# LayerNorm, V and output projection, weight quantizer and x loads in the first stage of a transformer layer: other slots

## The chip, the cores and the metric

One Trainium2 chip, all 8 cores. Each core computes 8192 of the 65,536 tokens by itself, with its own copy of the weights; the cores exchange nothing. The metric is the device time in microseconds of the slowest core. The kernel before took 3341.05 us (median of 3 runs, 3340.89 to 3342.73).

## The reference, cut to what matters

One layer: LayerNorm, attention in windows of 128 tokens (each window sees itself and the one before), residual, LayerNorm, a gated FFN whose activations and weights are rounded to FP4 in blocks of 16.

```python
x = x + _L0_attn_ref(_layernorm(x), wq, wkv, wo, bo)
x = x + _L0_ffn_ref(_layernorm(x), w_gate, w_up, w_down)

def _L0_attn_ref(x, wq, wkv, wo, bo):        # H = 16 heads of 64, W = 128
    q = x @ wq;  k, v = split(x @ wkv, 2)
    # windows of 128; keys and values of the window before are put in front
    sim = einsum('bwid,bwjd->bwij', qw, kw) * 64 ** -0.5, causal mask
    out = einsum('bwij,bwjd->bwid', softmax(sim), vw)
    return out @ wo + bo

def fp4_quant_dequant(x):                    # blocks of 16
    scale = max(max(abs(xb)) / 6.0, 1e-12)
    q = _GRID[searchsorted(_MID, abs(xb / scale))] * sign * scale
def _L0_ffn_ref(x, w_gate, w_up, w_down):    # 1024 -> 2816 -> 1024
    h = silu(q(x) @ q(w_gate).T) * (q(x) @ q(w_up).T)
    return q(h) @ q(w_down).T
```

## The kernel before

Every engine has its own stream of instructions, in the order in which the Python code calls it. A token (semaphore, count) stands for an instruction that has ended; an instruction that needs tokens waits at the head of its engine's queue, and all behind it wait too. DMAs are issued from two queues: SP (plain loads and DMA transposes) and POOL (weight loads that turn float32 into bf16, and stores). The DMA queues are in order as well: a DMA whose token is missing holds the issue of all behind it.

`attention` runs first, then a fence, then `ffn`. The change touches `attention` alone. It handles 64 tiles T of 128 tokens in 16 chunks of 4 tiles (`cc`), and in each chunk 8 pairs of heads (`p`). One pass of the loop over `n = 8 * cc + p` is called a slot here: 128 slots and one more to drain. In a slot TensorE (PE) does for pair n: scores of two half chunks (L536 to L549), the Q and K projection of pair n+1 (L440), softmax weights times V of pair n-1 (L600, L602), and two groups of eight 512-column matmuls (L440) called `extra`: the V projection of a tile of the next chunk (`proj_v`, drained by ACT in L483) or the output projection of a tile of the chunk before (`proj_o`, drained by DVE in L495). VectorE (DVE) does the row maxima (L558, two in a slot, so the first of them marks a slot's start), drains K (L468), divides (L610, L613) and rounds weights. ScalarE (ACT) does the exponentials (L566), drains Q (L457) and V, and most of LayerNorm. SP transposes the softmax weights P (`turn_p`, L574), the attention output (`turn_ao`, L622) and normalized x (`turn_x`, L409) by DMA.

LayerNorm of a tile (LN1): `load_x` (L340) into one of two buffers, `square_sum` (L384) and `plain_sum` (L391) on ACT, `scalars` on POOL (11 small instructions for two tiles, L286 to L301), `normalize` (L402) on ACT, `turn_x` on SP. In chunk cc the tiles of chunk cc+2 are loaded and summed and two of them normalized; the other two are normalized in slots 0 and 1 of the next chunk. Tiles 0 to 7 are done ahead of slot 0.

The residual: `load_xr` (L503) loads x once more, `add_bo` (L510) adds the bias on POOL, `proj_o` adds the product, and POOL stores to `x1s` in DRAM (L498). Two buffers; `load_xr(T)` waits for the store of tile T-2.

The weight quantizer (`rounding`) rounds the FFN's weights during the attention stage: 136 jobs of 5 steps, 7 DVE instructions (L228 to L273) and an ACT square (L253) each, a load by SP (L638) and a store by POOL (L672). `fill(share)` runs it up to that share of its 680 steps: 3% ahead of slot 0, and from there in equal parts, five calls of `upto` in a slot, up to slot 126.

## Time and profile before

| | us |
|---|---|
| median of 3 runs | 3341.05 |
| the profiled execution | 3333.16 |
| its span, slowest core (core 6) | 3331.5 |
| spans of the 8 cores | 3320.3 to 3331.5 |
| attention, from the span's start to the last matmul of it | about 1389 |
| PE busy over the span | 2984.4 (90%) |
| DVE busy over the span | 2787.0 (84%) |
| ACT busy over the span | 1535.0 (46%) |

The profile is one execution on the slowest core. Each engine's busy time is the sum of its instructions; "idle before" names what ended the wait. A matmul's recorded end is modelled, so a group of PE instructions that waits in its middle can look long and not idle. The granted clock is the share of TensorE's 2.4 GHz that the chip gave in that stretch: 1.00 is 2.4 GHz, 0.50 is 1.2 GHz, and what lies between is a mixture of the two. All times below are microseconds from the span's start.

### The profile page before, as it was taken

The page shows a single profiled execution, that of the slowest core. Times are in us where ns is not written, and L with a number is a line of the kernel's source. Part 1 is how long each engine was busy: PE and PEld are TensorE (multiplying, and loading weights), DVE is VectorE, ACT ScalarE, POOL GpSimd, SP SyncE. Part 2 cuts the span into 40 slices and gives each one's busy share as a digit, 9 for nine tenths or more (in the row PEclk, how much of TensorE's full clock was granted, in tenths as well). Part 3 has the DMA queues.
Part 4 walks back from the last instruction along what each step waited for, and adds up shares of the span by engine and source line. Part 5 has one row for each costly group of instructions (what it writes and reads, how often), then busy time and mean ns, then how long its engine had stood idle before and what let it go on. Part 6 is the DMA issues. An engine that isn't in the chain of part 4 may idle for free.

```text
span 3331.5 us, 53061 instructions; the slowest of 8 cores (3320.3 to 3331.5 us)
## 1 busy us (share of the span) xinstructions
PE 2984.4 (90%) x16413; PEld 1407.5 (42%) x16736; DVE 2787.0 (84%) x4992; ACT 1535.0 (46%) x3018; POOL 1190.0 (36%) x1912
## 2 busy tenths in 40 slices
PE   2888888888899998438999999999999999999997
PEld 1333443344444444114444444444444444444443
DVE  1888888888888889239999999999999999999984
ACT  3666665566666664124343433433333443343331
POOL 2123222222223232214444444444444444444431
PEclk7899999999999999769999999999999999999998
DMA  9689888888888987765333333333333333333322
GB/s 175 146 194 197 203 189 189 190 197 195 198 204 200 205 198 171 175 128 127 88 93 93 93 90 87 88 93 93 93 87 93 87 90 93 93 93 87 88 77 71
DMA packets 818805, 445.59 MB, mean 134 GB/s; under 512 B 736352, under 2 KB 747616, under 8 KB 818528
## 3 DMA queue, kind: packets, MB, share of 16 engines
q1 hardware_dynamic: 782112, 348.83, 47.9%
q0 software_dynamic: 36416, 93.34, 9.2%
q8 instruction: 140, 2.29, 0.3%
q14 instruction: 137, 1.12, 0.1%
HBM read 186.19 MB, written 84.41 MB: 81 GB/s over the span
## 4 chain that ended last, share of the span: by engine, by line
PE 65%; DVE 11%; DMA 7%; SPq 7%; issue 5%; ACT 3%; POOL 2%; POOLq 0%; ACTq 0%; DVEq 0%
PE ps L914 35%; PE ps L928 18%; PE ps L440 10%; DMA bfar<-bfar 5%; DVE far L558 2%; ACT bfar L566 2%; DVE far L259 1%; SPq L622 1%; SPq L574 1%; DVE far L495 1%; DVE bfar L273 1%; SPq L859 1%; DVE far L246 1%; SPq L861 1%; DVE bfar L613 1%
## 5 line engine op out<-in xcount | busy, mean ns | idle before, releaser
L914 PE MATMUL ps<-bfar 128*128 128x512 bf16 x6016 | 1250.8, 362 | 102.3 <-DMA bfar<-bfar 90.0
L440 PE MATMUL ps<-bfar 128*128 128x512 bf16 x3949 | 978.8, 389 | 156.0 <-ACT bfar L457 76.4
L914 PEld LDWEIGHTS ps<-bfar 128*128 128x128 bf16 x6144 | 602.1, 98 | 729.0 <-issue 103.9
L1037 POOL TENSOR_TENSOR bfar<-bfar,far 128x512 bf16<-128x512 bf16 (+1 forms) x512 | 503.2, 1002 | 955.7 <-DVE far L1020 952.0
L928 PE MATMUL ps<-bfar 128*128 128x512 bf16 x2768 | 646.0, 380 | 8.4 <-DVE far L1052 5.9
L440 PEld LDWEIGHTS ps<-bfar 128*128 128x128 bf16 x4096 | 386.4, 99 | 552.9 <-issue 198.4
L952 ACT ACTIVATE far<-ps 128x512 f32<-128x512 f32 (+1 forms) x384 | 214.0, 557 | 848.8 <-PE ps L914 828.7
L566 ACT ACTIVATE bfar<-ps,far 128x256 bf16<-128x256 f32 x1024 | 423.2, 478 | 341.6 <-DVE far L558 341.2
L928 PEld LDWEIGHTS ps<-bfar 128*128 128x128 bf16 x2816 | 276.0, 98 | 327.2 <-issue 10.1
L969 ACT ACTIVATE far<-far 128x512 f32<-128x512 f32 (+1 forms) x512 | 289.8, 599 | 267.4 <-DVE far L1020 267.4
L993 DVE TENSOR_REDUCE far<-far 128x32 f32<-128x512 f32 (+1 forms) x512 | 308.3, 642 | 68.7 <-ACT far L959 68.7
L986 DVE TENSOR_TENSOR far<-far,ps 128x512 f32<-128x512 f32 (+1 forms) x384 | 238.0, 635 | 149.7 <-PE ps L914 145.7
L510 POOL TENSOR_TENSOR far<-far 128x1024 f32<-128x1024 f32 x64 | 154.3, 2411 | 572.6 <-DMA far<-x 416.3
L558 DVE TENSOR_REDUCE far<-ps 128x4 f32<-128x1024 f32 x256 | 311.4, 1216 | 16.9 <-PE ps L549 16.7
L1008 DVE SCALAR_TENSOR_TENSOR far<-far 128x512 f32<-128x512 f32 (+1 forms) x512 | 317.3, 660 | 0.0
L1015 DVE SCALAR_TENSOR_TENSOR bfar<-far 128x512 bf16<-128x512 f32 (+1 forms) x512 | 311.6, 649 | 0.0
L1020 DVE SCALAR_TENSOR_TENSOR far<-far 128x512 f32<-128x512 f32 (+1 forms) x512 | 311.4, 648 | 0.0
L259 DVE SCALAR_TENSOR_TENSOR far<-far 128x512 f32<-128x512 f32 (+1 forms) x136 | 111.5, 820 | 42.5 <-ACT far L253 42.2
L1003 DVE RECIPROCAL far<-far 128x64 f32<-128x64 f32 (+1 forms) x256 | 135.1, 528 | 8.8
L600 PE MATMUL ps<-bfar 128*128 128x65 bf16 x1024 | 97.9, 195 | 44.8 <-DMA bfar<-bfar 44.5
L228 DVE TENSOR_REDUCE far<-far 128x32 f32<-128x512 f32 (+1 forms) x136 | 89.8, 660 | 46.9 <-DMA far<-wgate 41.1
L495 DVE TENSOR_TENSOR far<-far,ps 128x512 f32<-128x512 f32 x128 | 86.8, 680 | 40.0 <-PE ps L440 20.8
(68 smaller groups left out, 2618.6 us busy)
## 6 DMA issues: line engine op xcount, KB each, us to landing
far<-x SPq DMA_DIRECT2D x128, 512.0 KB, 5.0
far<-x1s SPq DMA_DIRECT2D x128, 512.0 KB, 3.7
x1s<-far POOLq DMA_DIRECT2D x64, 512.0 KB, 3.9
out<-far POOLq DMA_DIRECT2D x64, 512.0 KB, 3.0
far<-wgate SPq DMA_DIRECT2D x44, 256.0 KB, 3.7
far<-wup SPq DMA_DIRECT2D x44, 256.0 KB, 4.0
bfar<-bfar SPq DMA_TRANSPOSE x700, 3.9
far<-wdown SPq DMA_DIRECT2D x40, 256.0 KB, 3.7
```

Of the source, the lines that this page charges most:

```text
L440: ins = e.matmul(c.p(col, [[1, 512]]), lhs(k), rhs(k), start=(k == 0), stop=(k == 7))
L558: t_max[(n, hf)] = dve.step(lambda e: e.tensor_reduce(out=c.f(NM + s * 4, [[1, 4], [1, 1]]), in_=c.p(PS_S + hf * 1024, [[256, 4], [1, 256] ...
L566: t_exp[(n, hf)] = act.step(lambda e, i=i: e.activation(out=c.b(A_P + s * 1024 + i * 256, [[1, 256]]), in_=c.p(PS_S + hf * 1024 + i * 256, ...
L914: ins = e.matmul(c.p(col, [[1, nw]]), c.b(xo + k * 128, [[1, 128]]), c.b(woff + k * FI + ns, [[1, nw]]), start=(k == 0), stop=(k == 7))
L928: ins = e.matmul(c.p(col + half * 512, [[1, 512]]), c.b(ho + k * 128, [[1, 128]]), c.b(WDQ + k * DM + half * 512, [[1, 512]]), start=(k == ...
L969: done_sq[sl] = act.step(lambda e, i=i, nw=nw: e.activation(out=c.f(Q_W + i * 512, [[1, nw]]), in_=c.f(Q_V + i * 512, [[1, nw]]), func=AF. ...
L986: t_h[n] = tok[i] = dve.step(lambda e, n=n, i=i, nw=nw, sl=sl: e.tensor_tensor(out=source(sl, i, nw, False), in0=c.f(G_SG + (n % 2) * 512, ...
L993: tok[i] = dve.step(lambda e, i=i, sl=sl: e.tensor_reduce(out=c.f(am + i * 32, [[1, nbs[i]], [1, 1]]), in_=source(sl, i, nbs[i] * 16, True ...
L1008: shifted[i] = dve.step(lambda e, i=i, nw=nw: e.scalar_tensor_tensor(out=c.f(Q_S + i * 512, [[1, nw]]), in0=c.f(Q_W + i * 512, [[1, nw]]), ...
L1015: done_r[sl] = dve.step(lambda e, i=i, nw=nw: e.scalar_tensor_tensor(out=c.b(F_R + i * 512, [[1, nw]]), in0=c.f(Q_W + i * 512, [[1, nw]]), ...
L1020: done_v[sl] = dve.step(lambda e, i=i, sl=sl: e.scalar_tensor_tensor(out=c.f(Q_V + i * 512, [[16, nbs[i]], [1, 16]]), in0=source(sl, i, nb ...
L1037: done_q[sl] = pool.step(lambda e, i=i, dst=dst, psc=psc, pb=pb: e.tensor_tensor(out=c.b(dst, [[16, pb], [1, 16]]), in0=c.b(F_R + i * 512, ...
```

## The change

Five things are edited, all in `attention`.

1. Ahead of slot 0 only tiles 0 to 3 are normalized. Tiles 4 to 7 (chunk 1) and 8, 9 (half of chunk 2) are summed and normalized in slots 0 to 5 of chunk 0, by a table (`plan`). All of x's tiles 4 to 7 are loaded ahead of slot 0, tiles 6 and 7 into the residual buffers.
2. The quantizer starts with slot 6 and ends with slot 126 as before.
3. The load of wo moves from the start to the end of slot 2.
4. `proj_v` moves from slots 0, 1, 4, 5 of a chunk to 1, 4, 5, 7, and `proj_o` from 2, 3, 6, 7 to 2, 3, 6 and slot 0 of the next chunk. `normalize` of slots 0 and 1 goes from the slot's middle to its end, and the transpose of a chunk's tile 1 from the end of slot 7 to the middle of slot 0.
5. The loads are dealt out, one in a slot: `load_x` in slots 0, 2, 4, 6 (before: 0, 1, 4, 5), `load_xr` in 1, 3, 5, 7 (before: 0, 1, 4, 5).

```diff
+    def aside(T):
+        return T in (2, 3, 6, 7)
     def load_x(T):
-        sem = s_x[T] if T in (2, 3) else s_x[T % 2]
-        free = t_xn.get(T - 4 if T in (4, 5) else T - 2) if T >= 4 else None
+        sem = s_x[T % 2 + 2 * aside(T)]
+        free = None if T < 4 else t_xn[T - 4] if T < 10 else t_xn[T - 2]
...
-    t_wo_w = load_w(A_WO, d["wo"], 0, DM, DM, s_c[3])
+    t_wo_w = {}
...
     for T in range(4):
         normalize(T)
         turn_x_pe(T)
-        if T < 2:
-            load_x(T + 4)
+        load_x(T + 4)
...
-    for T in (4, 5):
-        square_sum(T)
-        plain_sum(T)
-    scalars(4)
-    for T in (4, 5):
-        normalize(T)
-        turn_x(T)
-        load_x(T + 2)
-    for T in (6, 7):
-        square_sum(T)
-        plain_sum(T)
-    scalars(6)
-    head = 0.03
-    fill(head)
+    quiet = 6
...
-            fill(head + (1 - head) * min(1.0, (n + part) / (n_units - 2)))
+            fill(min(1.0, (n + part - quiet) / (n_units - 2 - quiet)))
...
-        if more and p in (0, 1, 4, 5):
-            T = base1 + {0: 0, 1: 1, 4: 2, 5: 3}[p]
+        if more and cc >= 1 and p in (1, 4, 5, 7):
+            T = base1 + {1: 0, 4: 1, 5: 2, 7: 3}[p]
             extra = [(proj_v, T, 0), (proj_v, T, 1)]
-        if live and p in (2, 3, 6, 7) and cc >= 1:
-            T = base1 - 8 + {2: 0, 3: 1, 6: 2, 7: 3}[p]
+        if live and p in (2, 3, 6) and cc >= 1:
+            T = base1 - 8 + {2: 0, 3: 1, 6: 2}[p]
             extra = [(proj_o, T, 0), (proj_o, T, 1)]
+        if p == 0 and cc >= 2:
+            extra = [(proj_o, base1 - 9, 0), (proj_o, base1 - 9, 1)]
         if p in (2, 3) and cc == 0:
             extra = [(proj_v, 2 * p - 4, 1), (proj_v, 2 * p - 3, 1)]
+        if p >= 4 and cc == 0:
+            extra = [(proj_v, p, 0), (proj_v, p, 1)]
...
+        if cc == 0 and live:
+            plan = {0: ((4,), (5,)), 1: ((), (6,)), 2: ((7,), ()), 3: ((), (8,)), 4: ((9,), ())}
...
+            if p in (1, 3, 5):
+                middle.append(lambda T=2 * p + {1: 2, 3: 0, 5: -2}[p]: rows(T, T + 1))
...
+            if p == 2:
+                t_wo_w[0] = load_w(A_WO, d["wo"], 0, DM, DM, s_c[3])
...
-        if ahead and p in (0, 1):
-            load_x(base2 + p)
-        if ahead and p in (4, 5):
-            load_x(base2 + p - 2)
+        if ahead and cc >= 1 and p % 2 == 0:
+            load_x(base2 + p // 2)
...
-        if live and p in (0, 1, 4, 5) and cc >= 1:
-            T = base1 - 8 + {0: 0, 1: 1, 4: 2, 5: 3}[p]
-            load_xr(T)
-            add_bo(T)
+        if live and p in (1, 3, 5, 7):
+            T = base1 - 8 + {7: 4, 1: 1, 3: 2, 5: 3}[p]
+            if 0 <= T < n_tiles - 4:
+                load_xr(T)
+                add_bo(T)
```

How the instructions stand on three engines. The changed kernel's lines lie 2 further down from L340 on (L558 is L560 there). VectorE at the start, from the drains of the transposed x tiles (L425) and of the first K projection (L468) on, before:

```order
L425 CAST bfar<-ps 128x8x128 x4
L468 CAST bfar<-ps 128x512
L228 TENSOR_REDUCE far<-far 128x32
L234 TENSOR_SCALAR far<-far 128x32
L240 RECIPROCAL far<-far 128x32
L246 SCALAR_TENSOR_TENSOR far<-far 128x512
...
L273 TENSOR_TENSOR bfar<-bfar,far 128x512
L558 TENSOR_REDUCE far<-ps 128x4
```

and now:

```order
L427 CAST bfar<-ps 128x8x128 x4
L470 CAST bfar<-ps 128x512
L560 TENSOR_REDUCE far<-ps 128x4
L470 CAST bfar<-ps 128x512
L560 TENSOR_REDUCE far<-ps 128x4 x2
L612 RECIPROCAL far<-ps 128x4
L615 TENSOR_TENSOR bfar<-ps,far 128x256
```

31 instructions of the quantizer stood ahead of the first row maximum; none does now.

SP from the end of a chunk's last slot into the next chunk's first two, in mid-stream (L409 the transposes of x, L340 and L503 the loads of x, L574 and L622 the transposes of P and of the attention output, L638 the quantizer's loads), before:

```order
L409 DMA_TRANSPOSE bfar<-bfar 128x8x128 x2
L574 DMA_TRANSPOSE bfar<-bfar 128x8x128
L622 DMA_TRANSPOSE bfar<-bfar 128x2x128
L574 DMA_TRANSPOSE bfar<-bfar 128x8x128
L622 DMA_TRANSPOSE bfar<-bfar 128x2x128
L638 DMA far<-wup 128x512
L409 DMA_TRANSPOSE bfar<-bfar 128x8x128
L340 DMA far<-x 128x1024
L503 DMA far<-x 128x1024
```

and now:

```order
L411 DMA_TRANSPOSE bfar<-bfar 128x8x128
L505 DMA far<-x 128x1024
L576 DMA_TRANSPOSE bfar<-bfar 128x8x128
L624 DMA_TRANSPOSE bfar<-bfar 128x2x128
L411 DMA_TRANSPOSE bfar<-bfar 128x8x128
L640 DMA far<-wup 128x512
L576 DMA_TRANSPOSE bfar<-bfar 128x8x128
L624 DMA_TRANSPOSE bfar<-bfar 128x2x128
L411 DMA_TRANSPOSE bfar<-bfar 128x8x128
L342 DMA far<-x 128x1024
```

One transpose of x now stands where two stood, the second comes behind the slot's first pair of transposes, and one load of x stands in a slot instead of two.

ScalarE in the first slot of a chunk (L566 exponentials, L457 drain of Q, L402 normalize, L483 drain of V, L253 the quantizer's square), before:

```order
L566 ACTIVATE bfar<-ps,far 128x256 x2
L457 ACTIVATE bfar<-ps 128x512
L566 ACTIVATE bfar<-ps,far 128x256 x2
L402 ACTIVATE bfar<-far 128x1024
L566 ACTIVATE bfar<-ps,far 128x256 x2
L483 ACTIVATE bfar<-ps 128x8x64
L566 ACTIVATE bfar<-ps,far 128x256 x2
L483 ACTIVATE bfar<-ps 128x8x64
```

and now:

```order
L568 ACTIVATE bfar<-ps,far 128x256 x2
L459 ACTIVATE bfar<-ps 128x512
L568 ACTIVATE bfar<-ps,far 128x256 x2
L253 ACTIVATE far<-far 128x256
L568 ACTIVATE bfar<-ps,far 128x256 x4
L404 ACTIVATE bfar<-far 128x1024
```

Normalize has moved from ahead of the second half's exponentials to behind them, and the two drains of V have left the slot: it holds an output projection now, which VectorE drains.

## Rows read from the trace of the kernel before

**Rows 1.** Windows: engine busy time by stretch, granted clock, DMA share, GB/s

```profile
core 6: us, PE busy (x) PEld busy (x) DVE busy (x) ACT busy (x) POOL busy (x), PEclk, DMA share, GB/s
36.50:95.60 59.10, 4.78 (x29) 2.11 (x30) 17.61 (x35) 13.56 (x24) 9.29 (x26) 0.56 1.04 157
...
163.80:1286.00 1122.20, 1001.56 (x6624) 456.40 (x6751) 962.43 (x1718) 696.03 (x1502) 321.43 (x525) 0.98 0.87 196
```

**Rows 2.** Timeline, 41 to 96: start, us, engine, line, count [idle before]

```profile
47.06 6.35 SPq L409 DMA_TRANSPOSE bfar<-bfar  x1
...
75.09 0.69 DVE L228 TENSOR_REDUCE far<-far 128x32 f32<-128x512 f32 x1 [38.64 <-DMA far<-wgate]
...
92.92 1.21 DVE L558 TENSOR_REDUCE far<-ps 128x4 f32<-128x1024 f32 x1
...
95.64 0.58 PE L440 MATMUL ps<-bfar 128*128 128x512 bf16 x1 [54.21 <-ACT bfar L457]
```

**Rows 3.** DMA issues: transposes at 44.8 and 47.1, wo at 11.0; last number: landing

```profile
bfar<-bfar SPq DMA_TRANSPOSE x1, 11.5
...
bfar<-bfar SPq DMA_TRANSPOSE x1, 23.1
...
bfar<-wo POOLq DMA_DIRECT2D x1, 2048.0 KB, 76.5
```

**Rows 4.** Timeline of VectorE's row maxima, start of slots 1 and 2

```profile
102.88 1.22 DVE L558 TENSOR_REDUCE far<-ps 128x4 f32<-128x1024 f32 x1 [2.75 <-PE ps L549]
...
111.57 1.22 DVE L558 TENSOR_REDUCE far<-ps 128x4 f32<-128x1024 f32 x1 [0.25 <-PE ps L549]
```

**Rows 5.** Waits, 164 to 1300: total us, times, longest

```profile
ACT bfar L566 <- DVE far L558: 300.9, 185, 5.3
...
PE ps L440 <- DMA bfar<-bfar: 41.4, 13, 5.3
DVE far L259 <- ACT far L253: 41.4, 32, 3.0
```

**Rows 6.** Timeline, slot 48 (first of chunk 6) and start of slot 49

```profile
574.18 3.52 SPq L409 DMA_TRANSPOSE bfar<-bfar  x2
...
579.07 3.22 PE L440 MATMUL ps<-bfar 128*128 128x512 bf16 x8 [2.79 <-DMA bfar<-bfar]
...
585.28 1.22 DVE L558 TENSOR_REDUCE far<-ps 128x4 f32<-128x1024 f32 x1 [0.47 <-PE ps L549]
...
588.89 0.57 SPq L340 DMA_DIRECT2D far<-x  x1
```

**Rows 7.** Lines of the quantizer on VectorE, 164 to 1286: busy us, mean ns

```profile
L259 DVE SCALAR_TENSOR_TENSOR far<-far 128x512 f32<-128x512 f32 x118 | 99.5, 843 | 41.4 <-ACT far L253 41.4
L246 DVE SCALAR_TENSOR_TENSOR far<-far 128x512 f32<-128x512 f32 (+1 forms) x117 | 97.5, 833 | 0.0
...
L273 DVE TENSOR_TENSOR bfar<-bfar,far 128x512 bf16<-128x512 bf16 x117 | 86.2, 736 | 0.2 <-DMA wgqs<-bfar 0.2
L266 DVE SCALAR_TENSOR_TENSOR bfar<-far 128x512 bf16<-128x512 f32 x117 | 80.5, 688 | 0.0
L228 DVE TENSOR_REDUCE far<-far 128x32 f32<-128x512 f32 x117 | 77.2, 660 | 5.6 <-DMA far<-wup 4.6 <-DMA far<-wdown 1.0
...
L240 DVE RECIPROCAL far<-far 128x32 f32<-128x32 f32 (+1 forms) x117 | 39.3, 336 | 0.0
...
L234 DVE TENSOR_SCALAR far<-far 128x32 f32<-128x32 f32 (+1 forms) x117 | 28.3, 242 | 0.0
```

**Rows 8.** ScalarE's sum in slot 51 (began 606.4); landing of 52 x loads

```profile
609.53 1.08 ACT L384 ACTIVATE bfar<-far 128x1024 bf16<-128x1024 f32 x1
...
DMA to landing us min/median/max: 3.8/4.7/6.4
```

**Rows 9.** VectorE while POOL adds the bias (POOL L510 from 648.01 to 650.35)

```profile
648.14 2.75 DVE L259 SCALAR_TENSOR_TENSOR far<-far 128x512 f32<-128x512 f32 x1
```

**Rows 10.** The chain that ended last, at the attention stage's end

```profile
1371.39 4.98 DMA x1s<-far
```

More of the change, by code:

```diff
@@ L748, in attention @@
             extra = [(proj_o, T, 0), (proj_o, T, 1)]
+        if p == 0 and cc >= 2:
+            extra = [(proj_o, base1 - 9, 0), (proj_o, base1 - 9, 1)]
         if p in (2, 3) and cc == 0:
             extra = [(proj_v, 2 * p - 4, 1), (proj_v, 2 * p - 3, 1)]
-        first = second = None
-        if ahead and p in (2, 3, 6, 7):
-            T = base2 + {2: 0, 3: 1, 6: 2, 7: 3}[p]
-            first, second = (lambda T=T: square_sum(T)), (lambda T=T: plain_sum(T))
-        if ahead and p in (4, 5):
-            first = lambda T=base2 + p - 4: normalize(T)
@@ L780, in attention @@
             turn_ao(n - 1, 0)
-        if first:
-            first()
+        if more and p == 0 and cc >= 1:
+            turn_x(base1 + 1)
+        for part in middle:
+            part()
         upto(0.4)
```

51 lines of the change are left out of this document (38 added, 13 removed).

## The prediction

> **What bounds the kernel now.** I read the windows first, then the timeline at the start, then the waits and one chunk's first slot.
>
> Two places matter. The first is the start. PE waits 54.21 us, from 41.4 to 95.64, when slot 0's scores are all done [rows 2]. It is laid to a drain of Q on ACT, but the row above says who was late: VectorE waited 38.64 us, until 75.09, for the quantizer's first load. The first row maximum stands behind 31 quantizer instructions, and DVE came to it at 92.92. ACT sat on the sums of tiles 6 and 7 meanwhile, and SP took 6.35 us to issue one transpose of x. All of it stands in a flood of weight loads: the DMA share is 1.04 from 36.5 to 95.6, PE is busy 4.78 of 59.1 us there and its clock is 0.56 [rows 1].
>
> The second is the steady part. From 163.8 to 1286.0, 14 chunks or 112 slots, a slot takes 1122.2 / 112 = 10.02 us. PE is busy 1001.56 / 112 = 8.94 of that, and DVE 962.43 / 112 = 8.59 [rows 1]. The slots of chunk 0 that wait for nothing take 111.57 - 102.88 = 8.69 us [rows 4], and they run as fast as PE can go with all four groups of eight matmuls. So both engines are nearly full, PE a little ahead, and 1.3 us of each slot is waiting. The largest wait of PE with one cause is 41.4 us in 13 waits for a transpose [rows 5]. Rows 6 show one: in a chunk's first slot two transposes of x take SP 3.52 us to issue, `proj_v` of tile 0 waits 2.79 us for the first of them, and its eight matmuls then take 3.22 us.
>
> **The change, part by part.**
>
> *The start.* Gone from ahead of slot 0 are 31 DVE instructions and their wait, eight sums and two normalizes on ACT, two transposes of x on SP. The first row maximum then waits for PE's scores alone, and slot 0 starts near 37 (5 us ahead of where PE ran dry), 56 us earlier. What comes in its place is DMA. P's transposes of slots 0 and 1 are issued in the flood, where transposes landed after 11.5 and 23.1 us [rows 3]; in the quiet a slot has about 8 us for one. wo landed last, 76.5 us after 11.0, at 87.5. It is one of four weights of one size, so without it the flood should end near three quarters of that, 66 (an estimate). I let slot 1 wait until 52 for its first P (41 + 11.5), slots 1 and 2 end near 61 and 70, and slots 3 to 7 take 8.69 us each. ACT, which does eight tile sums and six normalizes in these slots now, hides them if it keeps up. wo's load, now beside the transposes of slots 3 and 4, costs perhaps 5 us, and the quantizer's first load holds DVE 4 us in slot 6 (a load of x of twice the size lands after 4.7, rows 8). Slot 8 then starts at 70 + 5 x 8.69 + 9 = 123; it started at 163.8, where the second row of rows 1 begins. That is -41, and I take -40. Bounds: with no wait at all, 37 + 8 x 8.69 = 106, or -58; with every P at 23.1 us until 87.5, then six slots and the 4 us, 144, or -20.
>
> *The quantizer.* Before, (0.03 + 0.97 x 8 / 126) x 680 = 62 steps are done when chunk 1 starts; now it is 2 / 120 x 680 = 11. So 51 steps, 10.2 jobs, move into chunks 1 to 15. A job is 0.843 + 0.833 + 0.736 + 0.688 + 0.660 + 0.336 + 0.242 = 4.34 us on DVE [rows 7]: +44 us of DVE work, 0.37 in a slot, which lifts DVE from 8.59 to 8.96, above PE's 8.69 floor. If DVE alone set the time, all 44 would show. If it fits into DVE's 1.43 idle us a slot, none. I take a third, 15, since DVE still has more idle time than it needs.
>
> *V and output projection turned, transposes spread.* In slot 0 of a chunk the extra groups are now an output projection whose inputs are a chunk old, so the 41.4 us of waits go. ACT's normalize no longer stands ahead of the second half's exponentials. PE's clock gives more: eight matmuls took 3.22 us behind the wait of slot 48, where in rows 4 a slot with 32 of them and all its scores fits in 8.69. The mean clock of 0.98 over 1122.2 us is worth 22 us, most of it, I think, behind these waits. Together 64. But DVE idles in just that slot too, and it now gets the output projection's two drains there, so it becomes the late one. I take half, -32 (bounds: 0 and -64). Output projections also stood in pairs (2, 3 and 6, 7) and three of four now alternate with V; that is the reason why I take not less than half. Steady part: -32 + 15 = -17, bounds -64 and +44.
>
> *Loads dealt out.* The number is the same. Two 512 KB loads no longer meet in one slot, and the two bias additions that met in slot 6 part. One such addition held a DVE instruction of 0.69 us for 2.75 [rows 9]. The price per addition stays, so I count 0. The Trainium skill (SBUF — State Buffer, on the shared port pair) calls this an exclusive lock between GpSimd and a DVE instruction with two SBUF inputs, held for a whole instruction; the row agrees. It would make 56 additions cost the same wherever they stand, and the quantizer, 8% denser in a slot (126 / (0.97 x 120)), meets them a little more often.
>
> *The tail.* The output projection of tile 59 moves behind slot 127, so its store and the load of tile 61 come later. That store takes 4.98 us in the chain [rows 10]. PE waits there anyway: +2, bounds 0 and +5.
>
> Sum: -40 - 17 + 2 = -55. The profiled execution took 3333.16 us and would take 3278; it lies 7.9 below the median of the runs, 3341.05, against which the change is measured. That gives 3286.
>
> **Rivals.**
>
> *The steady part gives all.* PE's 64 us come back and the quantizer fits in DVE's idle time. For it: DVE idles 160 of 1122 us. Against: idle time stands in other slots than the added steps. -40 - 64 + 0 + 2 = -102, so 3239; I let it run from 3216 to 3262.
>
> *The start stays in the flood.* P's transposes take 23 us until the weights are in, and wo does it again in slots 3 to 5. The start gives 20, the steady part 10: 3311, from 3306 to 3334. For it speaks the 23.1 us, against it that little but P is on that queue now.
>
> *DVE sets the steady part.* What is gained in slot 0 is paid in the others: -40 + 44 - 0 + 2 = +6, 3347, and with a little gained 3334: no difference that counts. For it: DVE is at 8.96 of a slot. Against: PE's waits were real and DVE had idle time beside them.
>
> *Late x loads, slower.* `load_x` of tiles 1 and 3 now stands at the end of slots 2 and 6, and their sums in the middle of 3 and 7, half a slot behind instead of one and a half. The load at the end of slot 48 was issued 3.6 us into slot 49 [rows 6] and lands 4.7 later, at 8.3; the sum started 3.2 into its slot [rows 8]. ACT, in order, would wait 5.1 us, with the second half's exponentials and the quantizer's square behind it, on which DVE waits (32 such waits before, rows 5). ACT's own wait for DVE at that place is 300.9 / 185 = 1.6 us, so 3.5 us pass on, twice in each of 13 chunks: +91. With -40 at the start, -32 and +15 this is +34, or 3375. It decides from the point where the load lands 4.8 us or more into the slot and DVE has no other work ready; below 2.2 us passed on, the change still gains. Against it: SP was late because slots 1, 2, 5 and 6 had two loads and a transpose each, and it now has one; with SP in time the load lands at 5.
>
> *The change does not do what it says.* The order on three engines shows that it does; I give this nothing.
>
> **How the numbers follow.** Forecast (3262 to 3306, with 3286 in it): 0.47. All of the steady part: 0.20. Start in the flood: 0.18. DVE sets it: 0.07. Late loads: 0.08. A measurement of this kernel tells about 0.2%, 6.7 us, from no change. Faster than that are the first three, and a little of them is lost at the edge to the fourth: 0.85. Same 0.07, slower 0.08. Range 3232 to 3330: it leaves out the lowest part of the second case, the DVE case and the late loads, about 2 in 10. The likeliest case's own range is 3262 to 3306.
>
> **What would show it.** Right: no PE wait over 15 us between 36 and 110; the ninth slot begins at 115 to 135; chunks 1 to 14 take 78 to 80 us each instead of 80.2 (1122.2 / 14); PE's waits for transposes in L442 fall from 41.4 to below 10; the clock of that stretch is 0.99. Wrong: ACT waits for `far<-x` by tens of us (late loads); DVE busy above 93% with slots at 10 us (DVE sets it); P's landing above 15 us until 90 (flood). If chunks take 76 us or less, I have priced the turned projections too low.

## The result and the profile after

The changed kernel took 3356.48 us (median of 5 runs, 3353.68 to 3364.3), the kernel before 3342.73 on the same chip. The ratio is 1.0046, 95% interval 1.0032 to 1.0059. The change made the kernel slower, by 15 us in 3342; the forecast was 3286, and a slower kernel had been given 8 in 100. Some executions run at a lower granted clock on half of the chip or on all of it; those cores are left out throughout.

Where the time went, from the first row maximum of each slot, mean of the 8 cores (worked out from both traces):

```
us                       before    after   difference
slot 0 begins              92.6     39.5     -53.1
slot 8 begins             162.2    142.3     -19.9
slots 8 to 120           1115.5   1150.7     +35.2
slots 120 to 127           56.8     62.9      +6.1
slot 127 to the FFN       127.6    128.0      +0.4
the rest (FFN)           1864.2   1865.7      +1.5
span                     3326.3   3349.6     +23.3
```

The sum is 23 and not 15 mainly because the profiled execution of before (3333.16) lay 10 us below its median. Slots 8 to 120 are chunks 1 to 14; they are called the steady part below. The windows of the changed kernel's slowest core, in the columns of [rows 1]: the first row is its first chunk, the second the steady part.

```profile
39.98:144.70 104.72, 70.68 (x440) 31.73 (x447) 41.06 (x71) 59.40 (x123) 9.79 (x35) 0.82 0.89 141
144.70:1300.90 1156.20, 1002.25 (x6625) 454.24 (x6753) 1005.04 (x1784) 697.80 (x1511) 329.53 (x535) 0.98 0.88 193
```

PE does the same work as in [rows 1] (1002 us); DVE has 43 us more, as forecast (44), and the stretch is 34 us longer. It moves at 193 GB/s what before moved at 196.

**The start.** PE's long wait of [rows 2] is gone: slot 0's row maximum stands at 40.02. The lengths of slots 0 to 7 are now (us, mean of the 8 cores, worked out from the traces):

```
slot         0     1     2     3     4     5     6     7
before     9.5   8.7   8.8   9.0   8.7   8.7   8.8   7.4
after      5.2  16.7  15.2  21.1   8.9   8.7  18.1   9.0
```

The flood of transfers shows in three places. In slots 1 and 2 P's transposes run beside the weights that are still under way; in slot 3 they run beside wo. Two windows of DMA issues (last number: median us from issue to landing), answering [rows 3]:

```profile
bfar<-bfar SPq DMA_TRANSPOSE x3, 11.3
...
bfar<-wo POOLq DMA_DIRECT2D x1, 2048.0 KB, 19.8
bfar<-bfar SPq DMA_TRANSPOSE x3, 17.2
```

The first row is 43 to 52 us, the last two are 73 to 83, behind wo's issue at 73.27. PE's waits for P from 36 to 110 us:

```profile
PE ps L602 <- DMA bfar<-bfar: 23.7, 3, 11.4
```

The third place is slot 6 (timeline; start, us, engine):

```profile
118.01 2.39 SPq L342 DMA_DIRECT2D far<-x  x2
...
120.44 9.52 SPq L640 DMA_DIRECT2D far<-wgate  x3
...
127.54 0.69 DVE L228 TENSOR_REDUCE far<-far 128x32 f32<-128x512 f32 x1 [10.48 <-DMA far<-wgate]
...
131.45 3.57 PE L442 MATMUL ps<-bfar 128*128 128x512 bf16 x8 [9.34 <-DVE bfar L470]
```

The quantizer's first load was issued behind two loads of x, DVE came to it 10.48 us too early, and PE waited for the drain of a projection (L470) that stood behind it. PE's eight matmuls then took 3.57 us instead of 1.89 elsewhere in the trace: the granted clock from 131.4 to 135.1 us was 0.50, that is 1.2 GHz, behind the wait of 9.34 us, and 1.00 from 110 to 118, where PE was busy 7.89 of 8 us. Over the whole first chunk it was 0.82.

**The steady part.** Waits of the changed kernel, 145 to 1300 (total us, times, longest), answering [rows 5]:

```profile
ACT bfar L568 <- DVE far L560: 323.9, 164, 6.7
...
DVE far L259 <- ACT far L253: 71.6, 44, 5.4
...
ACT far L253 <- DVE far L246: 56.8, 29, 4.7
PE ps L602 <- DMA bfar<-bfar: 53.5, 33, 4.6
...
ACT bfar L386 <- DMA far<-x: 39.7, 24, 3.7
```

PE's wait of 41.4 us for transposes of x (L440, now L442) is gone from the list, as foreseen. In its place DVE waits for ACT's square 71.6 us instead of 41.4, ACT for DVE's row maxima 323.9 instead of 300.9. In the mean of the 8 cores PE waits 141 us in all instead of 107: for P's transposes 53 instead of 34, for ACT's drains 60 instead of 27, for DVE 28 instead of 4. By place in the chunk (mean us of the slot, chunks 2 to 14) the time moved as well: before 11.80, 9.43, 10.30, 9.91, 8.69, 9.10, 11.21, 8.95; after 10.35, 9.22, 13.39, 9.62, 10.58, 8.78, 11.27, 9.13. Slot 0 of a chunk gained 1.5, slots 2 and 4 lost 5.0. In slot 2 PE now waits 2.2 us for P's transposes where it waited 0.5.

### The profile page after: what moved, and what is told of

Same layout as the page of the kernel before. It is cut to its first block, busy times and chain, and to the rows that moved or that the text cites. A ratio compares the mean times of both kernels' runs of the same rounds, so it can differ in the third digit from the quotient of the medians.

```text
span 3354.9 us, 53089 instructions; the slowest of 8 cores (3341.2 to 3354.9 us)
## 1 busy us (share of the span) xinstructions
PE 2991.7 (89%) x16414; PEld 1408.0 (42%) x16736; DVE 2799.6 (83%) x4992; ACT 1530.6 (46%) x3018; POOL 1190.8 (35%) x1912
## 4 chain that ended last, share of the span: by engine, by line
PE 63%; DVE 11%; DMA 9%; SPq 7%; issue 5%; ACT 4%; POOL 2%; POOLq 0%; ACTq 0%; DVEq 0%
PE ps L937 35%; PE ps L951 18%; PE ps L442 9%; DMA bfar<-bfar 4%; DMA far<-x 3%; DVE far L560 2%; ACT bfar L568 2%; DVE far L259 1%; SPq L624 1%; DVE far L246 1%; SPq L576 1%; DVE far L497 1%; SPq L884 1%; DMA bfar<-wq 1%; SPq L882 1%
## 5 line engine op out<-in xcount | busy, mean ns | idle before, releaser
L442 PE MATMUL ps<-bfar 128*128 128x512 bf16 x3950 | 976.3, 388 | 122.7 <-ACT bfar L459 30.9
L937 PEld LDWEIGHTS ps<-bfar 128*128 128x128 bf16 x6144 | 602.3, 98 | 735.3 <-issue 110.8
L1060 POOL TENSOR_TENSOR bfar<-bfar,far 128x512 bf16<-128x512 bf16 (+1 forms) x512 | 503.2, 1002 | 957.6 <-DVE far L1043 953.9
L442 PEld LDWEIGHTS ps<-bfar 128*128 128x128 bf16 x4096 | 384.4, 99 | 523.7 <-issue 167.3
L951 PEld LDWEIGHTS ps<-bfar 128*128 128x128 bf16 x2816 | 276.1, 98 | 327.5 <-issue 10.4
L1016 DVE TENSOR_REDUCE far<-far 128x32 f32<-128x512 f32 (+1 forms) x512 | 308.3, 642 | 72.9 <-ACT far L982 72.8
L560 DVE TENSOR_REDUCE far<-ps 128x4 f32<-128x1024 f32 x256 | 311.1, 1216 | 14.3 <-PE ps L551 14.2
L1031 DVE SCALAR_TENSOR_TENSOR far<-far 128x512 f32<-128x512 f32 (+1 forms) x512 | 317.3, 660 | 0.0
L1043 DVE SCALAR_TENSOR_TENSOR far<-far 128x512 f32<-128x512 f32 (+1 forms) x512 | 311.6, 648 | 0.0
L259 DVE SCALAR_TENSOR_TENSOR far<-far 128x512 f32<-128x512 f32 (+1 forms) x136 | 118.8, 873 | 73.6 <-ACT far L253 73.3
L1026 DVE RECIPROCAL far<-far 128x64 f32<-128x64 f32 (+1 forms) x256 | 135.1, 528 | 8.8
L602 PEld LDWEIGHTS ps<-bfar 128*128 128x128 bf16 x1024 | 81.4, 99 | 130.8 <-issue 107.5
L470 DVE CAST bfar<-ps 128x512 bf16<-128x512 f32 x128 | 87.6, 684 | 45.3 <-PE ps L442 44.7
```

The source lines that it names most:

```text
L442: ins = e.matmul(c.p(col, [[1, 512]]), lhs(k), rhs(k), start=(k == 0), stop=(k == 7))
L560: t_max[(n, hf)] = dve.step(lambda e: e.tensor_reduce(out=c.f(NM + s * 4, [[1, 4], [1, 1]]), in_=c.p(PS_S + hf * 1024, [[256, 4], [1, 256] ...
L937: ins = e.matmul(c.p(col, [[1, nw]]), c.b(xo + k * 128, [[1, 128]]), c.b(woff + k * FI + ns, [[1, nw]]), start=(k == 0), stop=(k == 7))
L951: ins = e.matmul(c.p(col + half * 512, [[1, 512]]), c.b(ho + k * 128, [[1, 128]]), c.b(WDQ + k * DM + half * 512, [[1, 512]]), start=(k == ...
L1016: tok[i] = dve.step(lambda e, i=i, sl=sl: e.tensor_reduce(out=c.f(am + i * 32, [[1, nbs[i]], [1, 1]]), in_=source(sl, i, nbs[i] * 16, True ...
L1031: shifted[i] = dve.step(lambda e, i=i, nw=nw: e.scalar_tensor_tensor(out=c.f(Q_S + i * 512, [[1, nw]]), in0=c.f(Q_W + i * 512, [[1, nw]]), ...
```

## The experiments

"Steady" is the length of slots 8 to 120, mean of the 8 cores of the profiled execution, "DVE" its busy time in them, "rest" the difference, "slot 8" when that slot begins. Ratios are to the kernel before, measured on the same chip; "none": there is no ratio with an interval.

```
                steady    DVE   rest  slot 8   ratio [95%]
before          1115.5   958.0   158   162.2   1
after           1150.7   997.5   153   142.3   1.0046 [1.0032, 1.0059]
e1_turns        1152.8   997.1   156   141.7   none
e2_loads        1144.2   981.9   162   142.7   none
e3_vo           1160.7   987.7   173   143.5   1.0072 [1.0023, 1.0122]
e4_quiet        1147.4   991.8   156   150.7   1.0063 [1.0035, 1.0091]
e5_head         1109.0   965.5   144   158.7   0.9963 [0.9946, 0.9980]
e6_wx           1150.6   995.6   155   134.9   none
e7_wo           1140.1   995.6   145   133.7   none
e8_put          1137.1   944.2   193   142.7   1.0005 [0.9982, 1.0027]
e9_thin         1136.9   938.4   199   142.6   none
e10_early       1123.1   967.3   156   142.7   0.9973 [0.9961, 0.9985]
e11_headmix     1108.2   950.1   158   158.3   0.9970 [0.9958, 0.9981]
e12_nosquare    1113.7  1003.9   110   141.0   none
e13_noload      1105.0   995.1   110   142.6   none
e14_order       1126.4  1029.3    97   140.7   none
e15_both        1117.6   976.9   141   154.4   none
```

Between cores of one run the steady part scatters by 12 to 26 us; of the means, a kernel without an edit there (e6_wx) came within 0.1 of the changed kernel, another (e7_wo) 10.6 below. So steady differences of up to about 10 us are not settled here. The rows come from several chips, one profiled execution each.

### One part undone at a time, one part alone

**e1_turns**: transposes of x both in slot 7, normalizes in the middle of slots 0 and 1.

```diff
-            ending.append(lambda T=base1 + 2 + p: rows(T))
+            middle.append(lambda T=base1 + 2 + p: rows(T))
...
-        if more and p == 0 and cc >= 1:
-            turn_x(base1 + 1)
...
             turn_x(base2)
+            turn_x(base2 + 1)
```

> The changed kernel, with LayerNorm's turns in a chunk's first slots as before: normalize of tiles 2 and 3 in the middle of slots 0 and 1, the transposes of tiles 0 and 1 together at the end of slot 7. The steady part (start of slot 8 to start of slot 120, mean of 8 cores) took 1115.5 us before and 1150.7 in the changed kernel, slot 2 of a chunk 10.3 and 13.4. Theory T (the turns: the transpose in the middle of slot 0 and the late normalize push P's transposes back on SP): the steady part falls by 25 or more, to 1125 or less, slot 2 to 11 or less. Theories Q (denser quantizer) and L (x loads half a slot ahead of their sum): both stay within 6 us of the changed kernel's.

1152.8 in the steady part: nothing (+2.1) either way. Slot 0 of a chunk got 1.2 us longer, slot 2 1.3 shorter, to 12.1.

**e2_loads**: `load_x` and `load_xr` of the changed kernel in slots 0, 1, 4, 5.

```diff
-        if ahead and cc >= 1 and p % 2 == 0:
-            load_x(base2 + p // 2)
+        if ahead and cc >= 1 and p in (0, 1, 4, 5):
+            load_x(base2 + {0: 0, 1: 1, 4: 2, 5: 3}[p])
...
-        if live and p in (1, 3, 5, 7):
-            T = base1 - 8 + {7: 4, 1: 1, 3: 2, 5: 3}[p]
+        if live and p in (0, 1, 4, 5):
+            T = base1 - 8 + {0: 0, 1: 1, 4: 2, 5: 3}[p]
```

> The changed kernel, with the loads as before: both loads of x in slots 0, 1, 4, 5. Theory L: ACT's waits for x (39.7 us in the changed kernel) go and the steady part falls by 15 or more from 1150.7. Theories T and Q: it stays within 6 us or rises, since SP gets two loads in slots 0 and 1 again; slot 2 stays at 13 or more.

1144.2, or -6.5, between the two forecasts; the dealt-out loads did not help and may have cost a little. ACT's waits for x went from 44 us to none in the mean of the cores, PE's for P rose from 53 to 74. DVE's busy time fell by 15.6 us (997.5 to 981.9), more than the whole: L259 ran beside a GpSimd operation of over 1 us 19 times a core instead of 29, and its mean fell from 876 to 808 ns.

**e3_vo**: V in slots 0, 1, 4, 5 and output projection in 2, 3, 6, 7, the rest as changed.

```diff
-        if more and cc >= 1 and p in (1, 4, 5, 7):
+        if more and cc >= 1 and p in (0, 1, 4, 5):
...
-        if live and p in (2, 3, 6) and cc >= 1:
+        if live and p in (2, 3, 6, 7) and cc >= 1:
...
```

> The changed kernel, with V in slots 0, 1, 4, 5 and the output projection in 2, 3, 6, 7 as before. A fourth theory V (the output projection in slot 0, whose store meets the transposes, makes slot 2 long): slot 2 falls below 11.5 and the steady part by 15 or more. Theory T: slot 2 stays at 13 or more, slot 0 gets its wait for the transposes of x back (10.35 to about 11.8), and the steady part rises by 10 or more. Q and L: the steady part rises by the wait in slot 0, 10 to 20.

1160.7: the turn is worth about 10 us of the 32 forecast, or less: on cores 2 and 3 the granted clock in these slots was 0.95 and 0.94, on the other six 0.97, against 0.98 in the changed kernel. Slot 0 is back at 12.97 us and slot 2 at 10.95 (13.39 in the changed kernel). The waits say what the turn did. With it undone PE waits 41.9 us for transposes of x and 11.2 for those of P; in the changed kernel it waits 0 and 53.0. The wait for the transposed x did not go away, it became a wait for P, two slots later.

**e4_quiet**: the kernel before with the quantizer alone changed.

```diff
-    head = 0.03
-    fill(head)
+    quiet = 6
...
-            fill(head + (1 - head) * min(1.0, (n + part) / (n_units - 2)))
+            fill(min(1.0, (n + part - quiet) / (n_units - 2 - quiet)))
```

> The kernel before, with one thing of the change: the quantizer starts with slot 6 and runs in equal parts up to slot 126, so each slot has 8% more of it. Theory Q: the steady part rises from 1115.5 by 20 or more (44 us of VectorE's work move into it). Theories T, L, V: by less than 8. In all of them slot 0 starts some 16 us sooner than before, since the quantizer's work ahead of it is gone.

The quantizer's shift alone gives 11.5 us at slot 8, costs 31.9 in the steady part, and the whole is slower by 0.63%. The steady part came as theory Q had it; the start did not. Slot 0 began at 37.6, 55 us sooner and not 16, but took 45.9 us: PE waited for a drain of Q that stood on ACT behind the sums of tiles 6 and 7, and these behind their loads of x. Core 3, 36 to 95 us:

```profile
PE ps L440 <- ACT bfar L457: 36.2, 1, 36.2
```

So the start needs both parts of the change: at slot 8 the quantizer's shift alone gives 11.5 us, the rest of the change without it 3.5 (e5_head), both together 19.9. The steady part of core 3; in the kernel before this core took 1113.90 us with 954.74 on DVE:

```profile
151.30:1296.10 1144.80, 1013.82 (x6755) 456.13 (x6754) 993.70 (x1786) 703.71 (x1509) 328.72 (x536) 0.97 0.88 195
```

**e5_head**: the changed kernel with the opposite edit.

> The changed kernel with one part undone: the weight quantizer begins in slot 0 with the share it had before the change (3 in 100 ahead of the loop, then evenly over the slots; 5.2 steps a slot instead of 5.7). Theory A (the denser quantizer costs what DVE works for it: DVE sets the slots of the steady part): slots 8 to 120 fall from 1150.7 us in the changed kernel to 1115 to 1122; the start gets longer, because the quantizer's first weight loads and steps wait in the flood of transfers again: slot 8 begins at 150 to 163 instead of 142.3; so the whole lies within 15 us of the changed kernel. Theory B (the turned projections, the turned transposes and the dealt-out loads made the slots longer and the quantizer fills gaps): slots 8 to 120 stay at 1140 or more.

1109.0, 41.7 us less: theory A's direction, 6 us beyond its range, for 32 us less work on DVE. The window of core 3:

```profile
159.30:1275.90 1116.60, 1005.44 (x6757) 454.54 (x6756) 961.70 (x1714) 692.46 (x1502) 322.84 (x525) 0.98 0.96 197
```

The start gives back 16.4. All the other parts together then make the kernel 0.37% faster than before; the quantizer's shift turns that into 0.46% slower. By both runs, one on each kernel, it is the part that decided the sign.

### The first chunk

**e6_wx**: the first two weight loads at the end of slot 4.

```diff
-        load_wx(0); load_wx(1)        # in rounding(), slot 6
...
+            if p == 4: load_wx(0); load_wx(1)
```

> The changed kernel with only the quantizer's first two weight loads issued at the end of slot 4, ahead of the loads of x tiles 10 and 11 and two slots before their use. If the 20 us of slot 6 come from DVE's wait for the first of them (10.5 us at 127.5 us in the changed kernel, with PE behind it for 9.3), slot 6 takes about 10 us, and slot 8 begins at 131 to 135 us instead of 142.3 in the mean of the cores. If the flood of transfers sets these slots as a whole, the wait only moves to another load and slot 8 stays within 4 us of 142. Slots 8 to 120 stay at 1150 plus or minus 4 by both.

**e7_wo**: wo in four pieces.

```diff
-            if p == 2: t_wo_w[0] = load_w(A_WO, d["wo"], 0, DM, DM, s_c[3])
+            if p in (2, 3, 4, 5):
+                t_wo_w[i] = load_w(A_WO + i * 256, d["wo"], i * 256, 256, DM, s_wo[i])
```

> The changed kernel with wo loaded as four transfers of 256 columns, one at the end of each of the slots 2 to 5, instead of one transfer at the end of slot 2. If the one large load of wo makes slot 3 22 us long (the transposes of P wait behind it for 12 to 18 us), slot 3 falls to 10 to 14 us, each of the slots 4 to 6 gains 0 to 3, and slot 8 begins at 132 to 137 us instead of 142.3. If only the number of bytes counts, the same time is spread over slots 3 to 6 and slot 8 stays at 140 to 144. Slots 8 to 120 stay as they are.

Both came as expected, but for e7_wo's steady part, which fell by 10.6 us without an edit there. Slot 6 fell from 18.1 to 11.5 us and slot 8 came 7.4 earlier; slot 3 fell from 21.1 to 14.0 and slot 8 came 8.6 earlier. The wait of core 4 in slot 6, in e6_wx:

```profile
DVE far L228 <- DMA far<-wgate: 1.2, 1, 1.2
```

and the pieces of wo with PE's waits for P from 60 to 110 us, in e7_wo (16.1 us in 2 waits in the changed kernel, longest 11.4):

```profile
bfar<-wo POOLq DMA_DIRECT2D x4, 512.0 KB, 9.5
...
PE ps L603 <- DMA bfar<-bfar: 11.4, 4, 4.1
```

### Is it DVE's work?

**e8_put**: L273 on GpSimd.

```diff
-        return c.dve.step(lambda e: e.tensor_tensor(
+        self.done[g] = c.pool.step(lambda e: e.tensor_tensor(
...
```

> The changed kernel with the last operation of each quantizer step group (the product of the rounded values with their scales, L273, 0.68 us on DVE, 127 times in slots 8 to 120, 86 us in all) done by GpSimd instead of DVE. Theory A (DVE sets the slots of the steady part; 34 to 40 us more work on it cost 32 to 35): DVE's busy time in slots 8 to 120 falls by 80 to 86 us and the slots by 60 to 80, from 1150.7 to 1070 to 1090; the whole from 3350 to 3270 to 3290. Theory B (the chain over PE and ACT sets them, DVE only follows): less than 20 us of it comes back. Theory C (GpSimd's operation of about 1 us on SBUF makes DVE's operations longer beside it, or it waits behind the add of bo, which waits for x, and holds DVE's rounding two jobs later): 20 to 50 us come back, and DVE's mean times of L246, L259 or L266 rise by over 5%, or a wait of DVE for GpSimd of tens of us appears.

1137.1: of 86 us taken off, DVE's busy time kept 33, and only 13.6 came back, as theory B had it. Theory C's mechanism is there beside it. Lines of e8_put, core 3, 145 to 1300 us:

```profile
L248 DVE SCALAR_TENSOR_TENSOR far<-far 128x512 f32<-128x512 f32 (+1 forms) x128 | 119.6, 934 | 0.9
L261 DVE SCALAR_TENSOR_TENSOR far<-far 128x512 f32<-128x512 f32 (+1 forms) x128 | 119.5, 933 | 81.5 <-ACT far L255 81.3
...
L276 POOL TENSOR_TENSOR bfar<-bfar,far 128x512 bf16<-128x512 bf16 x128 | 153.0, 1196 | 63.1 <-DVE far L616 33.5 <-DVE bfar L268 21.0 <-DMA wuqs<-bfar 3.8
```

GpSimd's operation takes 1196 ns. L248 and L261 took 934 and 933 ns where their twins in the changed kernel (L246 and L259) took 842 and 852 on the same core; in the mean of the 8 cores 891 and 903 instead of 814 and 876. DVE's wait for ACT's square grew too.

**e9_thin**: L273 on DVE, on 16 columns.

```diff
-            out=dst, in0=c.b(self.r_off + (g % 2) * 512, [[16, nb], [1, 16]]),
+            out=<first 16 columns of dst>, in0=c.b(self.r_off + (g % 2) * 512, [[16, 1], [1, 16]]),
```

> The changed kernel with the quantizer's last operation (L273) cut from 512 columns to its first 16, on DVE as before: the other 496 columns of each block of quantized weights are left out (a constant is stored there). It takes the same 86 us of DVE's work out of slots 8 to 120 as the kernel e8_put did, without giving GpSimd anything. Theory A (DVE's work sets the slots; GpSimd's operation beside it was what ate the gain of e8_put): DVE's busy time falls from 997.5 to 915 to 925 us and slots 8 to 120 from 1150.7 to 1070 to 1090. Theory B (DVE's work sets them only down to the next wait, for the transposes of P or for PE, some 15 to 40 us below): slots 8 to 120 stop at 1110 to 1137, and DVE's idle time in them grows from 153 us to 190 or more. Theory C (it is not DVE's work at all but the number of quantizer jobs, their loads and their waits for ACT): less than 12 us of change.

DVE lost 59 us of work and not the 73 to 82 expected, since L273 still takes 0.22 us on 16 columns. Again only 13.8 came back (theory B, at the edge of its range): DVE's idle time went from 153 to 199. So e8_put's missing gain was not GpSimd's doing in the main, and DVE's work alone does not set the slots. On core 4 DVE now waits 87.6 us for ACT's square (71.6 in the changed kernel) and PE 57.5 for P (53.5).

**e12_nosquare**: ACT's square left out, its readers read the ratio.

```diff
-                squares.append(lambda g=g, nw=nw: q.square(g, nw))
...
-            out=c.f(Q_S, [[1, nw]]), in0=c.f(Q_W + (g % 2) * 512, [[1, nw]]), scalar=LO_C,
+            out=c.f(Q_S, [[1, nw]]), in0=c.f(Q_V + (g % 2) * 512, [[1, nw]]), scalar=LO_C,
...
```

> The changed kernel without the quantizer's square on ACT: shift and round read the ratio in its place, so this part of the quantizer's formula is left out, but each DVE operation works on as many columns as before. DVE's work stays within 5 us of 997.5 in slots 8 to 120; ACT has some 80 us less. Theory R (a job costs its round trip: ACT's square waits for DVE's ratio, DVE's shift for ACT's square behind the exponentials; 71.6 us of waits of L259 and 56.8 of L253 on core 4): the shift's wait goes and slots 8 to 120 fall from 1150.7 to 1070 to 1110, DVE's idle time from 153 to 75 to 115 us. Theory D (the loads of the weights on SP's queue, ahead of the transposes of P) and theory W (DVE's work alone): less than 12 us come back.

1113.7: 37 us back with DVE's work unchanged (+6), 4 us short of the range. The mean span of cores 0 to 3 says the same: 0.994 of the kernel before here, 0.992 in e13_noload, where the changed kernel took 1.0046 of it by its slowest core.

**e13_noload**: loads of the weights left out from the third on.

```diff
-                if g + 2 < len(jobs):
-                    load_wx(g + 2)
```

> The changed kernel with the quantizer's loads left out from the third on: every job quantizes one of the first two blocks again, with the same work on DVE and ACT, the same stores and no load of 262 KB on SP's queue. Theory D (the loads delay the transposes of P, and PE's first matmul of the averages waits): slots 8 to 120 fall by 25 to 45 us to 1105 to 1125, and PE's wait of 53.5 us for the transposes (L602, core 4) falls below 25. Theory R: slots 8 to 120 fall by 0 to 12 us. In the first chunk slot 6 keeps its wait for the first load, slots 7 and 8 change little.

1105.0: 46 us back, with DVE and ACT as busy as in the changed kernel. The window of core 3, and PE's wait for P there (53.9 in the changed kernel's core 3):

```profile
141.10:1251.00 1109.90, 1000.42 (x6753) 452.73 (x6752) 993.87 (x1783) 696.90 (x1511) 327.96 (x535) 0.99 0.82 172
```

```profile
PE ps L602 <- DMA bfar<-bfar: 27.0, 19, 3.8
```

The same core of the changed kernel had a DMA share of 0.92:

```profile
141.30:1292.50 1151.20, 1008.27 (x6753) 452.96 (x6752) 996.89 (x1783) 698.90 (x1511) 331.86 (x535) 0.99 0.92 194
```

So theory D and theory R both hold, each for about 40 us. Neither explains the price of a job: they take a load or a square out of all 127 jobs of the steady part, 0.36 and 0.29 us each, and e9_thin most of an operation for 0.11. Together that is 97 us or 0.76 a job, while e5_head takes out 9.7 jobs, one in thirteen, and gives 41.7.

**e14_order**: one more step between ratio and shift (the order of the steps, in words).

```diff
-    amax | shift, of job g-1 | scale, round g-1 | recip, put g-1 | ratio
+    amax | scale, recip | shift g-1 | round g-1, put g-1 | ratio
```

> The changed kernel with the five steps of a quantizer job in another order: amax, scale with reciprocal, shift of the job before, its round and put, ratio. The same operations; between the ratio and the shift that needs its square lie two steps (1.3 us of DVE's work and on average a third of a slot more) instead of one. Theory R: the shift's wait for ACT (71.6 us on core 4) falls below 35 and slots 8 to 120 from 1150.7 to 1120 to 1138; the whole is 0.2 to 0.5% under the changed kernel and level with the one before. If the round trip costs by its mere presence (ACT in order, waiting for the ratio), or the step of 1.4 us with round and put holds the row maxima longer, less than 8 us come back.

1126.4: 24 us back, in the range of theory R. Cores 0 to 3 took 0.9975 of the kernel before in its six executions. Core 3, 145 to 1250 us: the shift's wait went from 74.8 us to 28.0, below. DVE's busy time rose by 32 us. Two things are in that. L240 and L273 now stand right behind the operation whose result they need, in each job, and L234 and L266 in one job of five. Where no long GpSimd operation runs beside them, the median from one operation's end to the next one's is then 0.13 us longer (L266: 598 ns behind L615, 726 behind L259, which it needs), about 307 times a core, or 39 us; against it L246 and L259 met long GpSimd operations less often (30 times a core instead of 46). The longer mean of L266 (691 to 823 ns) is something else: it met a GpSimd operation of over 1 us 15 times a core instead of 3; alone it takes 670 ns in both.

```profile
L266 DVE SCALAR_TENSOR_TENSOR bfar<-far 128x512 bf16<-128x512 f32 (+1 forms) x124 | 102.0, 823 | 1.0
...
L259 DVE SCALAR_TENSOR_TENSOR far<-far 128x512 f32<-128x512 f32 (+1 forms) x124 | 94.2, 759 | 28.0 <-ACT far L253 28.0
L273 DVE TENSOR_TENSOR bfar<-bfar,far 128x512 bf16<-128x512 bf16 (+1 forms) x123 | 93.8, 762 | 4.2
```

### Versions meant to beat both

**e10_early** takes e2_loads, e7_wo, `quiet = 2` and the first two weight loads at the end of slot 0:

> The changed kernel with four edits that are meant to beat both: the loads of x and of x for the residual in slots 0, 1, 4 and 5 as before the change, wo in four pieces at the ends of slots 2 to 5, the quantizer from slot 2 instead of 6 (5.48 steps a slot instead of 5.67), its first two loads at the end of slot 0. From the runs so far: slot 8 at 142.3 - 8.6 (wo) - 7.4 (first loads) + 6 (five more weight loads in the first chunk) = 132 us; slots 8 to 120 at 1150.7 - 6.5 (loads) - 18 (0.19 steps x 112 slots x 0.87 us) = 1126; mean span of the cores 3349.6 - 10 - 6.5 - 18 = 3315, so 0.4 to 0.6% faster than the kernel before. If the loads in the first chunk hold DVE as they did before the change, slot 8 begins at 145 or later and the gain is 0.2% or less.

The gain of 0.27% is below the 0.4 to 0.6 expected. The steady part is as worked out (1123.1 for 1126), slot 8 is not (142.7 for 132): with weight loads and steps in them, slots 2 to 4 took 18.8, 19.2 and 12.2 us where e7_wo took 14.9, 14.0 and 8.8.

**e11_headmix** takes e5_head, e2_loads and e7_wo:

> The kernel e5_head (the changed kernel with the quantizer from slot 0 as before the change, 5.2 steps a slot) with the loads of x in slots 0, 1, 4 and 5 as before the change and wo in four pieces. From the runs so far: slot 8 at 158.7 - 8 = 151 us, slots 8 to 120 at 1109 - 6.5 = 1102.5, mean span of the cores 3317.5 - 8 - 6.5 = 3303, that is 0.7 to 0.8% faster than the kernel before. If the loads in slots 0, 1, 4 and 5 help only where the quantizer is dense, slots 8 to 120 stay at 1109 and the span at 3310.

1108.2, no better than e5_head, as the second sentence had it, and the ratio of 0.9970 is e5_head's within the intervals. Slot 8 came no earlier either (158.3 for 158.7): slot 4 fell from 18.8 to 9.4 us, but slots 5 and 6 rose from 8.7 and 9.7 to 12.7 and 13.2.

**e15_both** adds the order of e14_order:

> The kernel e11_headmix (quantizer from slot 0 at 5.2 steps a slot, loads of x in slots 0, 1, 4, 5, wo in four pieces, the rest as changed) with the order of steps of e14_order. If the shift's wait is what can still be saved: slots 8 to 120 fall from 1108.2 to 1085 to 1100, the ratio to the kernel before from 0.997 to 0.990 to 0.995. If not, 0.996 to 0.998.

1117.6 instead of 1108.2: at 5.2 steps a slot the order gains nothing and may cost. Cores 0 to 3 took 0.9995 of the kernel before in five executions, outside both forecasts.

## Why the prediction was wrong

**The step that failed is the quantizer's term**: "If DVE alone set the time, all 44 would show. If it fits into DVE's 1.43 idle us a slot, none. I take a third, 15". The work was right: 44 us forecast, 32 to 40 found. What it cost was 31.9 us (e4_quiet, on the kernel before) and 41.7 (e5_head, undone in the changed one), near the upper bound, not a third. This term decided the sign: without it the kernel is 0.37% faster than before. Of the 70 us between forecast and measurement it is 17 to 27, the start 20, the turn 22 or more, the loads 6 and the tail 4. The reason given for a third was that DVE had more idle time than the steps need. It has, and it had as much afterwards (158 and 153 us): the idle time is made of waits that come with the work. A job brings a square on ACT between two DVE operations, and a load and a store on DMA engines that were at 0.90 of their time on core 3. The prediction priced a job by its 4.34 us on DVE and by nothing else. 9.7 more jobs in the steady part (0.432 steps x 112 / 5) at 31.9 to 41.7 us are 3.3 to 4.3 us each. That is close to the 4.34 us of DVE work, but DVE's work is not the reason: 53 and 59 us less of it gave 14 (e8_put, e9_thin).

How much of the price is DVE, ACT or DMA is not settled. The five calls of `upto` make most slots take five steps; a slot that takes a sixth does two of them at one place. Before, 26 of the 112 slots had a sixth step, now 74. Within a kernel one can ask what a slot with one more step takes. A least-squares fit of the slots' lengths in the changed kernel (104 slots, 8 cores, the mean of each place in the chunk taken off) gives, beside the DVE time of the step's operations:

```
step                    longer slot    on DVE
amax                        0.87        0.66
shift (waits for ACT)       2.16        0.89
scale and round             1.36        1.00
recip and put               1.18        1.01
ratio (ACT waits for it)    2.17        0.85
```

Each number of the first column is uncertain by about 0.4, and the fit explains only 28% of the scatter. The two ends of the round trip over ACT cost over twice their work. The same fit of e12_nosquare, which has no round trip, gives 0.34, 0.61, 0.75, 0.68 and 0.58, or 3.0 us a job instead of 7.7; that of e13_noload, which has no loads, still 6.2. So it is the round trip that makes an added step dear, as far as a fit can show it. The fit also makes a job dearer than any run did. Whether DVE with its round trip and the DMA engines are two bounds that lie close together, so that relieving one stops at the other, would show in a kernel with e9_thin's and e13_noload's edits at once; whether it is the place of a second step, in one with six places a slot. Neither was run.

**The start: -20, not -40.** The mechanism was right in the main: no wait of PE over 11.4 us, slot 0 at 40. But the prediction laid PE's long wait to DVE alone; with the quantizer gone from there (e4_quiet) the drain of Q on ACT still held PE for 36 us. Slot 1 ended at 61.4, as forecast (61), and the 19 us to 123 came in three slots behind it. Slot 2 took 15.2 us where 9 were forecast: P was still in the flood. Slot 3 took 21.1 and not 14: wo was to cost "perhaps 5 us", and in four pieces instead of one it already costs 8.6 less at slot 8. Slot 6 took 18.1 and not 13: the quantizer's first load was to hold DVE 4 us and held it 10.48, of which an earlier issue gives back 7.4 at slot 8; SP issued it behind two loads of x, and the 4.7 us of [rows 8] were those of the quiet part. Nor did the prediction count the clock, 0.82 in the first chunk. The start came out where the rival "start stays in the flood" had it (-20), which got 0.18. The Trainium skill (DMA: Bandwidth & Descriptors, Queues, rings and completion order) gave this end: each engine takes its queues in turn, packet by packet. The trace agrees where both queues had work: from 50 to 55, 55 to 60 and 85 to 90 us the weights' queue and the transposes' moved 1161 and 1160, 1218 and 1218, 393 and 393 packets. That was 0.59 against 0.29 MB in the first of them and 0.80 against 0.10 beside wo in the last.

**V and output projection turned: -10, not -32.** PE's 41.4 us of waits for transposes went, as said, and slot 0 of a chunk became 1.5 us shorter. Undoing the turn costs 10.0 (e3_vo), at the edge of what a steady part tells. The step that failed here is that these 41.4 us "go": they came back as waits for P, 53.0 us instead of 11.2 (e3_vo), most of it in slot 2. The prediction had counted on DVE to become late in slot 0 and took half for that; slot 0 did get shorter, and the loss stood in slot 2. The 22 us of clock did not come: the granted clock of the steady part is 0.98 in both kernels, where the prediction had 0.99.

**Loads dealt out: 0 forecast, +6.5 measured** (e2_loads), also at that edge. The late-load rival is there in kind and small in size: ACT waits for `far<-x` 39.7 us in 24 waits, the longest 3.7, not 5.1 twice in each chunk. With these waits gone the steady part fell by 6.5 us, so little of them passed on, and the rival was no part of the result's sign.

**The tail: +2 forecast**, +6.1 in slots 120 to 127. With the quantizer as before these slots are 3.3 us shorter (e5_head, 59.6), so it is half of that; the other half is not explained.

In the steady part and the singles: +41.7 (quantizer), -10.0 (turn), +6.5 (loads), -2.1 (transposes) make +36 of the 35.2 seen. That it fits so well is luck, since three of the four are no larger than what a steady part leaves unsettled, and the first is 31.9 by e4_quiet. Of the rivals "DVE sets the steady part" had the right size (+6, up to 3347, chance 0.07), though not for its reason. Of the signs named beforehand, two came: PE had no wait over 15 us, and its waits for transposes in L442 were gone. Those against the forecast came too: chunks took 82.2 us instead of 78 to 80, slot 8 was at 144.7 on the slowest core instead of by 135, ACT waited for x by tens of us, and P landed after 16.0 and 18.2 us twice before 90. "DVE busy above 93%" did not come (87%), and it was the wrong sign to look for.

## What to carry to other kernels

When background work moves onto an in-order engine that is at 86%, take the upper bound of its price, not a share of it, and look at its round trips to other engines and its transfers too: here 0.4 steps more in a slot cost 32 to 42 us, as much as the earlier start was to give (40). Idle time of an in-order engine is no room for more work until a run has shown that it is. A wait that is removed may come back at the next transfer in the same queue: 42 us of waits for x became 42 us more for P. If a start is crowded, move the work out of it only as far as the part that receives it has been shown to have slack; here the same edits without the quantizer's shift are 0.37% faster than before, and with it 0.46% slower.

## What the runs showed of the hardware

On DVE an operation starts about 83 ns before the recorded end of the one ahead, and 34 ns after it where it needs that one's result (medians of e14_order and the changed kernel, no long GpSimd operation beside them). From end to end this made L240 387 ns instead of 259 and L266 726 instead of 598, 0.13 us for each such pair. In the same two kernels L246, L259 and L266 took 1.3 to 1.7 us on average where they met a GpSimd operation of over 1 us, and 0.67 alone.

One transfer of 2 MB beside small transposes holds them more than four of 512 KB in four slots: slot 3 took 21.1 us with the one, 14.0 with the four, and slots 4 and 5 did not get longer. The product of 128x512 took 676 ns on DVE (core 4 of the changed kernel) and 1196 ns on GpSimd (e8_put).
